# Expert weights on the sync queue in the second mixture of a gated cross-attention stack

## The chip, the cores and the metric

The kernel runs on one core of a Trainium2 chip. The metric is device time in microseconds (us) of one execution. Before the change three executions took 871.26 us in the median (871.09 to 873.1).

## The reference

The program takes 8 sequences of 100 tokens, 256 features each (T = 800 tokens), and a context of 361 rows per sequence. It applies four parts in a row, each as `x = x + tanh(gate) * part(layernorm(x))`: a cross attention, a part with attention and a mixture of experts, another cross attention, and a second mixture of experts. Only the last is touched here:

```
d2 = |x|^2 + |centroid|^2 - 2 x centroid^T          # 8 experts
w, sel = top_k(sqrt(max(d2, 1e-12)), 2);  w = softmax(w)
for e in range(8):
    h = silu(x @ Wg[e] + bg[e]) * (x @ W1[e] + b1[e])      # 256 -> 684
    out = out + we[:, e] * (h @ W2[e] + b2[e])             # 684 -> 256
```

## The kernel before

Each of the five engines (TensorE, ScalarE, VectorE, GpSimd, and SyncE, called SP, which only starts transfers) runs a list of its own, written out by hand; counting semaphores order them. The second mixture is computed by need: a token is worked on only by its two experts.

**The blocks.** The pairs of token and expert are sorted into 20 blocks of 128 slots (`NBLK`), each for one expert. Blocks 0 to 7 belong to experts 0 to 7. The 12 others (`NOV`) go to experts with more than 128 tokens; their owners are known only when the router is done. `route` (from line 2112) and `owners` (line 2199) compute on VectorE the token of each slot (XROW, for reading), the row of the output (TROW, for adding) and the owners. Line 2205 writes into WROW, for each block and partition, the row number `128 * expert + partition` in the weight tables; line 2096 does so for blocks 0 to 7 from a constant.

**The data of a block.** The gate and up weights of an expert are 128 rows of 2,736 floats, 1.40 MB, held in one of three tiles RAW. ScalarE rounds them into GUH (`gu_high`, line 1349) and VectorE writes the rest into GUL (`gu_low`, line 2072), half a tile at a time. The down weights lie in the DRAM table as 128 rows of 1,536 floats per expert, of which 115 are used (114 rows of weights, one of bias); they go to one of two tiles DOWN. Token rows (128 of 1,024 B) are gathered from a DRAM copy into XB. Result rows, 128 of 1,024 B in one of two tiles YO, are added into the output in DRAM by an indirect transfer with addition.

**One turn of TensorE's loop** (line 1027), for block k: gate and up products of half 0 (`up1`, 14 products); three transposes of the hidden part of block k-1, half 1 (`turn_hidden`, line 1011); two transposes of the tokens of block k+1 (line 981); gate and up products of half 1; the down product of block k-1 (`down1`, line 1014, 6 products that the trace shows as 12 matmuls); three transposes of block k, half 0. `down1` waits for the hidden part, for the down tile (line 1017) and for the result rows of the block before to be out of PSUM (line 1018). All matmuls are recorded with line 468, that of a helper. VectorE scales the down product into YO (`rows_out`, line 2223), and before that waits until the added rows of two blocks before have landed.

**Who moves what.** SP loads statically: the router's constants, the weights of experts 0 to 2 and the down weights of expert 0 (lines 445 to 455; tiles 1 and 2 behind a wait for the mixed heads, line 449, and the biases behind these tiles, line 453); it stores the token rows (line 457) and the first output (line 459). All else of the mixture goes through GpSimd's queue, each as an indirect transfer: `gather_weights` (line 1538, rows by WROW), `gather_down` (line 1565, 115 rows by WROW), `gather_rows` (line 1570) and `add_rows` (line 1579). GpSimd's loop (line 1596) does for each k, in this order:

```
gather_rows(k + 3)        # waits until the token rows before have landed
wait until block k's weights are split;  gather_weights(k + 3)
add_rows(k - 1)           # waits for YO, and until the added rows before have landed (line 1582)
gather_down(k + 1)
```

So the down tile of block k+1 follows, in the program and in the queue, the added rows of block k-1, whose product was the last reader of the same tile.

Of the kernel before, what the change touches and what calls it, by code (L numbers as in the profile page):

```python
# [13 lines left out]
U32 = mybir.dt.uint32  # L14
ALU = mybir.AluOpType
# [4 lines left out]
B, S, D = 8, 100, 256  # L20
# [3 lines left out]
P = 128  # L24
# [9 lines left out]
E1, HID1 = 8, 684  # L34
# [3 lines left out]
HT1 = HID1 // 6  # L38
NBLK = (2 * T + E1 * P) // P
NOV = NBLK - E1  # L40
# [12 lines left out]
def program(nc, t):  # L53

    with ExitStack() as ctx:
# [6 lines left out]
        def part(name, shape, region, at, dt=F32R):  # L62

            return nc.alloc_sbuf_tensor_at(name, shape, dt, offset=base[region] + 4 * at)
# [11 lines left out]
        RB = sb("RB", [P, 11400])  # L76
# [138 lines left out]
        at_ = GU1  # L215
        ROUTE = cut(RB, at_, 568)
        LIMITS = ROUTE[:, 0:48].rearrange("p (e j) -> p e j", e=E1)
        BEFORE = ROUTE[:, 48:112].rearrange("p (e f) -> p e f", e=E1)
        SHIFT, BLOCK, TOKEN = ROUTE[:, 112:120], ROUTE[:, 120:120 + NOV], ROUTE[0:S, 132:140]
        LANE, UNITROW, FIRST = ROUTE[:, 140:141], ROUTE[:, 141:142], ROUTE[:, 142:150]  # L220
        STATIC, PICKED = ROUTE[:, 150:158], ROUTE[:, 158:166]
        STARTS, EMPTY = ROUTE[:, 166:166 + NBLK], ROUTE[:, 186:186 + NBLK]
        LANES, TRIANGLE = ROUTE[:, 206:206 + P], ROUTE[0:S, 334:334 + S + P]
        TMP = cut(RB, at_ + 568, 288)
# [1 line left out]
        FRONT, PAST = TMP[:, 64:128].rearrange("p (e f) -> p e f", e=E1), TMP[:, 128:136]  # L226
        PASSED, OWNER = TMP[:, 136:136 + NOV * E1].rearrange("p (k e) -> p k e", e=E1), TMP[:, 232:232 + NOV]
        VACANT, OFFSET = TMP[:, 244:244 + NBLK], TMP[:, 264:272]
        WROW = part("WROW", [P, NBLK], "RB", at_ + 856, U32)
        TROW = part("TROW", [P, NBLK], "RB", at_ + 880, U32)  # L230
        XROW = part("XROW", [P, NBLK], "RB", at_ + 904, U32)
        PICKB = part("PICKB", [P, NBLK], "RB", at_ + 928)
# [120 lines left out]
        def _(sp):  # L353
            def load(dst, src, name):
                sp.dma_start(dst, src).then_inc(sem[name], 16)
# [56 lines left out]
            def load_keys(b):  # L412
                sp.wait_ge(sem[f"c_keys_stored{b % 2}"], 16 * (b // 2 + 1))
                if b >= 3:
                    sp.wait_ge(sem["c_turned_scores_summed"], 12 * (b - 2))
                if b == 2:
                    sp.wait_ge(sem["c_query_turned_up"], 16)
                src = KSC[b % 2].rearrange("(p x) n c -> x p n c", x=32)
                for r, n in enumerate((0, 0, 1)):
                    load(KST[b % 3][32 * r:32 * r + 32, :, :].bitcast(F32), src[:, :, n, :], f"c_keys_loaded{b % 3}")  # L420
                rows = 5 if b < 3 else 1
                sp.wait_ge(sem["mask_stored"], 16)
                src = MSC[16 * b:16 * b + rows].unsqueeze(1).to_broadcast([rows, 8, KVE])
                load(KST[b % 3][96:96 + rows, :, :].bitcast(F32), src, f"c_keys_loaded{b % 3}")
# [15 lines left out]
            for b in range(B - 3):  # L440
                if b + 4 < B:
                    load_context(b + 4)
                store_keys(b + 3)
                load_keys(b + 3)
            load(ROUTE, t["route"], "moe1_small_loaded")
            load(RAW[0], t["W1"][0:P], "moe1_small_loaded")
            sp.wait_ge(sem["c_turned_scores_summed"], 12 * (B - 1))
            sp.wait_ge(sem["moe1_small_loaded"], 48)
            sp.wait_ge(sem["c_heads_mixed"], 4 * (B - 1))
            for k in (1, 2):  # L450
                load(RAW[k], t["W1"][k * P:(k + 1) * P], "moe1_small_loaded")
            sp.wait_ge(sem["c_turned_scores_summed"], 12 * B)
            sp.wait_ge(sem["moe1_small_loaded"], 80)
            load(BRAW, t["b1g"], "moe1_small_loaded")
            load(DOWN[0], t["W2"][0:P].rearrange("p (t c) -> p t c", t=6), "moe1_small_loaded")
            sp.wait_ge(sem["rows_copied"], 4)
            sp.dma_start(XROWS.rearrange("(b s) c -> s b c", s=S), ROWS[:, :, :]).then_inc(sem["rows_stored"], 16)
            sp.wait_ge(sem["moe_turned_copied"], 6)
            sp.dma_start(t["out"][0:T].rearrange("(b s) c -> s b c", s=S),
                         RESID[:, :, :]).then_inc(sem["out_stored"], 16)  # L460
            sp.wait_ge(sem["out_stored"], 16)
            sp.wait_ge(sem["rows_added"], 16 * NBLK)

# [2 lines left out]
        def _(pe):  # L466
# [546 lines left out]

            def down1(k):
                pe.wait_ge(sem["hidden_high_ready"], N0 + 2 * k + 2)
                if k:
                    pe.wait_ge(sem[f"down_loaded{k % 2}"], 16 * ((k + 1) // 2))
                    pe.wait_ge(sem["rows_out_ready"], k)
                else:
                    pe.wait_ge(sem["router_result_ready"], 8)  # L1020
                for x in range(6):
                    rows = HT1 if x else HT1 + 1
                    m = mm(PS[:, 7, 0:D], HTT1[0:rows, x, :], DOWN[k % 2][0:rows, x, :], x == 0, x == 5)
                m.then_inc(sem["down_summed"], 1)
# [18 lines left out]
        def _(act):  # L1043
# [297 lines left out]
                             PS[0:96, 4 + i % 3, 0:HALF]).then_inc(sem["c_query_stacked_even"], 1)  # L1341

            def weights_there(k):
                if k >= 3:
                    act.wait_ge(sem[f"weights_loaded{k % 3}"], 16 * (k // 3))
                else:
                    act.wait_ge(sem["moe1_small_loaded"], 80 if k else 48)

            def gu_high(k, j):
                weights_there(k)  # L1350
# [64 lines left out]
                         PS[0:HT1, 5 + j, 0:3 * P].rearrange("p (x c) -> p x c",  # L1415
                                                             x=3)).then_inc(sem["hidden_high_ready"], 1)

            act.wait_ge(sem["moe1_small_loaded"], 112)
            act.wait_ge(sem["zeros_set"], 7)
            act.copy(BROWS[0:40, 0:2 * HID1], BRAW).then_inc(sem["bias_rows_ready"], 1)  # L1420
            gu_high(1, 0)
# [31 lines left out]
        def _(pool):  # L1453
# [81 lines left out]
                                       COLS[0:96, 21 + u:22 + u].unsqueeze(2).to_broadcast([96, 8, S]),  # L1535
                                       ALU.mult).then_inc(sem["c_query_slots_ready"], 1)

            def gather_weights(k):
                pool.indirect_dma_start(RAW[k % 3], None, t["W1"],
                                        bass.IndirectOffsetOnAxis(ap=WROW[:, k:k + 1],  # L1540
                                                                  axis=0)).then_inc(sem[f"weights_loaded{k % 3}"], 16)

            pool.wait_ge(sem["zeros_set"], 6)
            for b in range(3):
                mask_queries(b)
# [16 lines left out]
            pool.wait_ge(sem["c_added_to_x"], 4)  # L1562
            pool.wait_ge(sem["zeros_set"], 7)
            pool.memset(HTT1[96:P, 0, :], 1.0).then_inc(sem["zeros_set"], 1)
            def gather_down(k):
                pool.indirect_dma_start(DOWN[k % 2][0:HT1 + 1].rearrange("p t c -> p (t c)"), None, t["W2"],
                                        bass.IndirectOffsetOnAxis(ap=WROW[0:HT1 + 1, k:k + 1],
                                                                  axis=0)).then_inc(sem[f"down_loaded{k % 2}"], 16)

            def gather_rows(k):  # L1570
                if k:
                    pool.wait_ge(sem["tokens_loaded"], 16 * k)
# [10 lines left out]
                pool.indirect_dma_start(t["out"], bass.IndirectOffsetOnAxis(ap=TROW[:, k:k + 1], axis=0),  # L1583
                                        YO[:, k % 2, :], None, compute_op=ALU.add).then_inc(sem["rows_added"], 16)

            pool.wait_ge(sem["expert_weights_low_ready"], N0 + 2)
            gather_weights(3)
            gather_down(1)
            pool.wait_ge(sem["rows_stored"], 16)
            pool.wait_ge(sem["router_result_ready"], 5)  # L1590
            gather_rows(0)
# [2 lines left out]
            pool.wait_ge(sem["router_result_ready"], 6)  # L1594
            pool.wait_ge(sem["out_stored"], 16)
            for k in range(NBLK + 1):
                if k + 3 == E1:
                    pool.wait_ge(sem["router_result_ready"], 9)
                if k + 3 < NBLK:
                    gather_rows(k + 3)  # L1600
                if k and k + 3 < NBLK:
                    pool.wait_ge(sem["expert_weights_low_ready"], N0 + 2 * k + 2)
                    gather_weights(k + 3)
                if k:
                    add_rows(k - 1)
                    if k + 1 < NBLK:
                        gather_down(k + 1)


        @block.vector  # L1610
        def _(dve):
# [465 lines left out]
            for q in range(-2, QUADS):  # L2077
                b, g = divmod(q, 4)
                ahead = q + 2 < QUADS
                if ahead:  # L2080
                    top(q + 2, 0)
                    top(q + 2, 1)
                if g == 1 and b >= 1:
                    outs(b - 1)
                if g in (1, 2) and 0 <= b and b + 3 < B:
                    keys_lo(b + 3, g - 1)
                if ahead:
                    top(q + 2, 2)
                    top(q + 2, 3)
                    split_maxima(q + 2)  # L2090
                if q < 0:
                    keys_lo(2, q + 2)
                if q == 24:
                    dve.wait_ge(sem["moe1_small_loaded"], 48)
                    dve.tensor_copy(PICKB[:, 0:E1], PICKED)
                    dve.tensor_copy(WROW[:, 0:E1], STATIC).then_inc(sem["router_result_ready"], 1)
                if q == -2:
                    stack_odd(1)
            outs(B - 1)
# [99 lines left out]
            def owners():  # L2199
                link(dve.tensor_tensor(PAST, PAST, FULL, ALU.add))  # L2200
                link(dve.tensor_tensor(PASSED, BLOCK.unsqueeze(2).to_broadcast([P, NOV, E1]),
                                       PAST.unsqueeze(1).to_broadcast([P, NOV, E1]), ALU.is_ge))
                link(dve.tensor_reduce(OWNER, PASSED, AX_X, ALU.add))
                link(dve.tensor_scalar(OWNER, OWNER, E1 - 1.0, None, ALU.min))
                dve.tensor_scalar(WROW[:, E1:NBLK], OWNER, float(P), LANE, ALU.mult,
                                  ALU.add).then_inc(sem["router_result_ready"], 1)
                dve.tensor_scalar(PICKB[:, E1:NBLK], OWNER, UNITROW, None,
                                  ALU.is_equal).then_inc(sem["router_result_ready"], 1)

# [183 lines left out]
```

## Time and profile before

| | us |
|---|---|
| median of three executions | 871.26 |
| the profiled execution, its own time | 877.44 |
| its span, first to last instruction | 875.6 |
| mean granted TensorE clock, share of full | 0.933 |

| engine | busy us | share of the span |
|---|---|---|
| TensorE, products (PE) | 760.1 | 87% |
| TensorE, weight loads (PEld) | 629.0 | 72% |
| VectorE (DVE) | 563.3 | 64% |
| ScalarE (ACT) | 415.0 | 47% |
| GpSimd (POOL) | 284.2 | 32% |

The second mixture begins with its router at about 643 us; its first product starts at 667.85 us. Transfers: GpSimd's queue carried 42.51 MB over the span, SP's 41.13 MB. "issue" as the end of an idle time means that the profile shows no releaser. "DMA share" is the mean busy share of the core's 16 DMA engines. "SPq" is SP's queue; the time beside an issue there is that of the issue, or, for merged ones, from the first to the last. "x12" counts instructions. A chain is followed back from the last instruction, at each step to what released it.

### The profile page before, as it was taken

Reading aid. Unit: us, or ns where it says so; the run is one execution under the profiler, and the core shown is the slowest. Engines: PE = TensorE matmul, PEld = TensorE weight load, DVE = VectorE, ACT = ScalarE, POOL = GpSimd, SP = SyncE. Lnnn points to the kernel's source line nnn. Section 1 sums busy time; section 2 is a strip of 40 time slices with the busy share of each in tenths; the row PEclk is TensorE's granted clock in tenths of the full one; section 3 lists DMA queues with packets and bytes.
Section 4 is the critical chain, followed back from the end, with each engine's and each line's share of the span. In section 5 each row is a group of like instructions: output and inputs, shape, how many; then the busy total and the mean of one; then the engine's idle time right before and its main releaser. Section 6 shows DMA issues by size and latency. Waiting matters only on the chain.

```text
span 875.6 us, 13584 instructions
## 1 busy us (share of the span) xinstructions
PE 760.1 (87%) x4761; PEld 629.0 (72%) x4761; DVE 563.3 (64%) x1031; ACT 415.0 (47%) x896; POOL 284.2 (32%) x231
## 2 busy tenths in 40 slices
PE   6999999998988399989988988888978988888894
PEld 3588888888944387479964766676558877778783
DVE  3369999998359799176665666765365644454540
ACT  4544444442342299254443565666472544453440
POOL 0074544440016234300033022240312454554632
PEclk9999999999999699879999999997876999998998
DMA  6400000000240000000007674350432689888862
GB/s 243 173 1 18 18 18 18 18 1 0 84 191 0 0 2 2 1 0 1 10 0 176 156 169 106 108 144 21 156 134 68 190 236 231 238 225 241 237 157 67
DMA packets 33610, 84.51 MB, mean 97 GB/s; under 512 B 8566, under 2 KB 24406, under 8 KB 30215
## 3 DMA queue, kind: packets, MB, share of 16 engines
q0 software_dynamic: 13584, 42.51, 17.8%
q1 hardware_dynamic: 19959, 41.13, 15.8%
q8 instruction: 40, 0.66, 0.3%
q14 instruction: 27, 0.22, 0.1%
HBM read 73.23 MB, written 10.38 MB: 95 GB/s over the span
## 4 chain that ended last, share of the span: by engine, by line
PE 56%; DVE 13%; issue 7%; ACT 4%; DMA 2%; POOL 1%; POOLq 0%; SPq 0%; DVEq 0%; ACTq 0%
PE PS L468 52%; DVE RW L1752 2%; PE PS L1011 1%; DVE SM L2050 1%; DVE WK L1812 1%; PE PS L640 1%; DVE WK L1809 1%; DVE RO L1755 1%; DMA KST<-mask_rows 1%; PE PS L857 1%; PE PS L981 1%; ACT SQ L1056 1%; ACT RO L1189 0%; POOL OT L1551 0%; DVE M L2059 0%
## 5 line engine op out<-in xcount | busy, mean ns | idle before, releaser
L1466 POOL TENSOR_TENSOR PRODL<-RW,PRODH 128x361 fp32r<-128x361 f32 x64 | 64.9, 1017 | 114.0 <-ACT PRODH L1123 110.4
L468 PE MATMUL PS<-CTXH,WKV0H 128*128 128x362 f32 x256 | 86.4, 338 | 9.6 <-DVE RW L1708 9.0
L2050 DVE TENSOR_REDUCE SM<-PS 100x1 f32<-100x362 f32 x128 | 64.8, 531 | 44.5 <-PE PS L468 43.8
L468 PE MATMUL PS<-RB,HTT 114*128 114x256 f32 (+1 forms) x240 | 65.4, 429 | 27.3 <-issue 24.8
L468 PE MATMUL PS<-CTXL,WKV0H 128*128 128x362 f32 x256 | 84.7, 331 | 0.0
L468 PE MATMUL PS<-CTXH,WKV0L 128*128 128x362 f32 x256 | 84.3, 329 | 0.0
L468 PEld LDWEIGHTS PS<-RB,HTT 114*128 114x128 f32 (+1 forms) x240 | 50.0, 214 | 38.7 <-issue 31.0
L1312 ACT ACTIVATE WK<-PS 120x400 f32<-120x400 f32 (+1 forms) x96 | 48.4, 507 | 40.9 <-PE PS L468 40.0
L468 PEld LDWEIGHTS PS<-CTXH,WKV0H 128*128 128x128 f32 x256 | 48.7, 190 | 15.9 <-DVE RW L1708 11.1
L468 PE MATMUL PS<-KST,QST 97*100 97x362 f32 x128 | 53.2, 428 | 6.3 <-DMA KST<-mask_rows 3.4
L1755 DVE TENSOR_REDUCE RO<-RW 128x100 f32<-128x400 f32 x64 | 56.2, 878 | 2.2
L1123 ACT CAST PRODH<-RW 128x361 fp32r<-128x361 f32 x64 | 31.8, 496 | 53.8 <-DVE RW L1708 53.5
L2074 DVE TENSOR_TENSOR GUL<-RB,GUH 128x1368 fp32r<-128x1368 f32 x28 | 44.1, 1578 | 14.3 <-ACT GUH L1353 14.3
L1115 ACT COPY RW<-PS 128x361 f32<-128x361 f32 x64 | 29.5, 463 | 49.2 <-PE PS L468 47.8
L1583 POOL DMA_INDIRECT out<-YO,TROW x20 | 32.2, 1608 | 62.3 <-DVE YO L2227 30.8
L1414 ACT COPY HTT<-PS 114x384 f32<-114x384 f32 x40 | 19.2, 483 | 69.4 <-PE PS L1011 69.4
L468 PE MATMUL PS<-GUH,XTH 128*128 128x342 f32 x160 | 51.9, 324 | 0.0
L468 PE MATMUL PS<-GUL,XTH 128*128 128x342 f32 x160 | 51.8, 324 | 0.0
L468 PE MATMUL PS<-GUH,XTL 128*128 128x342 f32 x160 | 51.6, 323 | 0.0
L1551 POOL TENSOR_TENSOR OT<-STD 128x400 f32<-128x400 f32 x8 | 11.2, 1397 | 117.8 <-ACT STD L1327 117.8
L468 PEld LDWEIGHTS PS<-CTXL,WKV0H 128*128 128x128 f32 x256 | 49.0, 192 | 0.0
L468 PEld LDWEIGHTS PS<-CTXH,WKV0L 128*128 128x128 f32 x256 | 48.8, 191 | 0.0
(314 smaller groups left out, 2041.1 us busy)
## 6 DMA issues: line engine op xcount, KB each, us to landing
KST<-keys_by_head SPq DMA_DIRECT2D x24, 362.0 KB
keys_by_head<-KTHL SPq DMA_DIRECT2D x8, 724.0 KB, 3.4
CTX<-ctxT SPq DMA_DIRECT2D x16, 361.0 KB, 6.7
RB<-W SPq DMA_DIRECT2D x2, 1368.0 KB
RW<-WGU SPq DMA_DIRECT2D x1, 2304.0 KB, 8.6
RW<-WKV SPq DMA_DIRECT2D x1, 2048.0 KB, 9.8
RQ<-W SPq DMA_DIRECT2D x1, 1368.0 KB
RW<-WD SPq DMA_DIRECT2D x1, 1152.0 KB, 10.2
```

Of the source, the lines that this page charges most:

```text
L468: return pe.matmul(out, lhsT, rhs, start=start, stop=stop)
L1115: act.copy(VSB[:, i % 3, 0:KV], PS[:, 4 + i % 2, 0:KV]).then_inc(sem["a_values_copied"], 1)
L1123: act.copy(PRODH[:, i % 4, 0:KV], PROD[:, i % 3, 0:KV]).then_inc(sem["a_products_high_ready"], 1)
L1312: act.activation(PTC[0:CHT[c], q % 2, c, :], PS[0:CHT[c], 2 + c, 0:4 * S], ACT.Exp).then_inc(sem["c_exp_taken"], 1)
L1414: act.copy(HTT1[0:HT1, 3 * j:3 * j + 3, :], PS[0:HT1, 5 + j, 0:3 * P].rearrange("p (x c) -> p x c", x=3)).then_inc(sem["hidden_high_ready" ...
L1466: pool.tensor_tensor(low, raw, high, ALU.subtract).then_inc(sem["a_products_low_ready"], 1)
L1551: pool.tensor_tensor(o, UN.rearrange("p (g c) -> p g c", g=4), SUMS.rearrange("p (g c) -> p g c", g=4), ALU.mult).then_inc(sem["c_mixed_bi ...
L1583: pool.indirect_dma_start(t["out"], bass.IndirectOffsetOnAxis(ap=TROW[:, k:k + 1], axis=0), YO[:, k % 2, :], None, compute_op=ALU.add).the ...
L1752: dve.tensor_tensor(PV[:, i % 2, :], PS[:, 6 + i % 2, 0:HALF], VSB[:, i % 3, :], ALU.mult).then_inc(sem["a_weighted"], 1)
L1755: dve.tensor_reduce(OT0[:, ti, tok(b)], PV[:, i % 2, :].rearrange("p (c i) -> p i c", c=NC), AX_X, ALU.add).then_inc(sem["a_heads_mixed"], 1)
L2050: dve.tensor_reduce(SM1[:, q % 2, j:j + 1], PS[0:S, i % 2, 0:KVE], AX_X, ALU.max, negate=True).then_inc(sem["c_maximum_found"], 1)
L2074: dve.tensor_tensor(GUL[k % 2][:, :, j, :], raw_gu(k, j), GUH[k % 2][:, :, j, :], ALU.subtract).then_inc(sem["expert_weights_low_ready"], 1)
```

## The change

All expert weights of the mixture are loaded by SP with direct transfers. For blocks 0 to 7 the address is static. From block 8 on SP reads the owner's number from SBUF into a register (`value_load`) ahead of each transfer, once for the weights and once for the down tile, and takes the 128 table rows of that expert. The down tile is loaded with all 128 rows. GpSimd's queue keeps the token rows and the added rows. WROW and its constants go; VectorE writes the owners' numbers as integers into OWNED. Each RAW and DOWN tile has its own semaphore from the first load on. The waits at lines 448, 449 and 453 go or become smaller, since the router's constants alone are behind `moe1_small_loaded` now. SP's loop waits for the split of block k+1 before weights k+4, and for the down product of block k-1 before down tile k+1.

```diff
@@ SP
+            def expert_rows(table, k):
+                if k < E1:
+                    return table[k * P:(k + 1) * P]
+                e = sp.value_load(OWNED[0:1, k - E1:k - E1 + 1], min_val=0, max_val=E1 - 1)
+                return table[bass.ts(e, P)]
+
+            def load_weights(k):
+                load(RAW[k % 3], expert_rows(t["W1"], k), f"weights_loaded{k % 3}")
+
+            def load_down(k):
+                load(DOWN[k % 2].rearrange("p t c -> p (t c)"), expert_rows(t["W2"], k), f"down_loaded{k % 2}")
+
             load(ROUTE, t["route"], "moe1_small_loaded")
-            load(RAW[0], t["W1"][0:P], "moe1_small_loaded")
+            load_weights(0)
             sp.wait_ge(sem["c_turned_scores_summed"], 12 * (B - 1))
-            sp.wait_ge(sem["moe1_small_loaded"], 48)
-            sp.wait_ge(sem["c_heads_mixed"], 4 * (B - 1))
-            for k in (1, 2):
-                load(RAW[k], t["W1"][k * P:(k + 1) * P], "moe1_small_loaded")
+            load_weights(1)
+            load_weights(2)
             sp.wait_ge(sem["c_turned_scores_summed"], 12 * B)
-            sp.wait_ge(sem["moe1_small_loaded"], 80)
+            sp.wait_ge(sem["moe1_small_loaded"], 32)
             load(BRAW, t["b1g"], "moe1_small_loaded")
-            load(DOWN[0], t["W2"][0:P].rearrange("p (t c) -> p t c", t=6), "moe1_small_loaded")
+            load_down(0)
+            load_down(1)
+            sp.wait_ge(sem["expert_weights_low_ready"], N0 + 2)
+            load_weights(3)
             sp.wait_ge(sem["rows_copied"], 4)
             sp.dma_start(XROWS.rearrange("(b s) c -> s b c", s=S), ROWS[:, :, :]).then_inc(sem["rows_stored"], 16)
             sp.wait_ge(sem["moe_turned_copied"], 6)
             sp.dma_start(t["out"][0:T].rearrange("(b s) c -> s b c", s=S),
                          RESID[:, :, :]).then_inc(sem["out_stored"], 16)
+            for k in range(NBLK - 1):
+                if k + 4 == E1:
+                    sp.wait_ge(sem["router_result_ready"], 9)
+                if k + 4 < NBLK:
+                    sp.wait_ge(sem["expert_weights_low_ready"], N0 + 2 * (k + 1) + 2)
+                    load_weights(k + 4)
+                if k:
+                    sp.wait_ge(sem["down_summed"], N0 + k)
+                    load_down(k + 1)
@@ TensorE, down1
+                pe.wait_ge(sem[f"down_loaded{k % 2}"], 16 * (k // 2 + 1))
                 if k:
-                    pe.wait_ge(sem[f"down_loaded{k % 2}"], 16 * ((k + 1) // 2))
                     pe.wait_ge(sem["rows_out_ready"], k)
@@ ScalarE
             def weights_there(k):
-                if k >= 3:
-                    act.wait_ge(sem[f"weights_loaded{k % 3}"], 16 * (k // 3))
-                else:
-                    act.wait_ge(sem["moe1_small_loaded"], 80 if k else 48)
+                act.wait_ge(sem[f"weights_loaded{k % 3}"], 16 * (k // 3 + 1))
@@ GpSimd (the functions gather_weights and gather_down are removed)
-            pool.wait_ge(sem["expert_weights_low_ready"], N0 + 2)
-            gather_weights(3)
-            gather_down(1)
             for k in range(NBLK + 1):
-                if k + 3 == E1:
-                    pool.wait_ge(sem["router_result_ready"], 9)
                 if k + 3 < NBLK:
                     gather_rows(k + 3)
-                if k and k + 3 < NBLK:
-                    pool.wait_ge(sem["expert_weights_low_ready"], N0 + 2 * k + 2)
-                    gather_weights(k + 3)
                 if k:
                     add_rows(k - 1)
-                    if k + 1 < NBLK:
-                        gather_down(k + 1)
@@ VectorE
-                    dve.tensor_copy(PICKB[:, 0:E1], PICKED)
-                    dve.tensor_copy(WROW[:, 0:E1], STATIC).then_inc(sem["router_result_ready"], 1)
+                    dve.tensor_copy(PICKB[:, 0:E1], PICKED).then_inc(sem["router_result_ready"], 1)
@@ VectorE, owners
-                dve.tensor_scalar(WROW[:, E1:NBLK], OWNER, float(P), LANE, ALU.mult,
-                                  ALU.add).then_inc(sem["router_result_ready"], 1)
+                dve.tensor_copy(OWNED[:, :], OWNER).then_inc(sem["router_result_ready"], 1)
```

## Rows read from the trace of the kernel before

**Rows 1.** The page: the span

```profile
span 875.6 us, 13584 instructions
```

**Rows 2.** Stretch: length, busy us of PE, PEld, DVE, ACT, POOL, clock, DMA share, GB/s

```profile
700.00:840.00 140.00, 117.96 (x661) 107.39 (x659) 66.63 (x82) 62.98 (x98) 75.35 (x55) 0.94 0.87 234
```

**Rows 3.** Chain that ended last, start and length in us: block turns, stalls, down products

```profile
682.93 0.33 PE PS L1011 x3
...
719.87 0.33 PE PS L1011 x3
...
725.13 2.54 issue
727.66 4.50 PE PS L468 x12
...
803.73 0.33 PE PS L1011 x3
...
806.80 4.78 PE PS L468 x26
811.59 0.33 PE PS L1011 x3
...
857.30 2.84 PE PS L468 x12
...
860.93 3.67 DMA out<-YO,TROW
```

**Rows 4.** Waits in 668 to 860 us; columns: total us, times, longest

```profile
PE PS L468 <- issue: 25.8, 15, 3.9
```

**Rows 5.** Timeline of GpSimd, one turn of its loop; idle before, and releaser, in brackets

```profile
720.12 0.94 POOL L1539 DMA_INDIRECT RQ<-W,WROW  x1 [0.30 <-issue]
722.90 1.62 POOL L1583 DMA_INDIRECT out<-YO,TROW  x1 [1.83 <-DMA out<-YO,TROW]
724.82 1.18 POOL L1566 DMA_INDIRECT RB<-W,WROW  x1 [0.30 <-issue]
```

**Rows 6.** DMA issues in 680 to 845 us; last column: median us from issue to landing

```profile
RB<-W,WROW POOLq DMA_INDIRECT x26, 12.1
out<-YO,TROW POOLq DMA_INDIRECT x16, 9.9
```

**Rows 7.** Stretches of 2 us, columns as in rows 2

```profile
614.00:616.00 2.00, 1.99 (x31) 1.85 (x32) 0.89 (x2) 1.19 (x2) 0.00 (x0) 0.75 1.02 425
638.00:640.00 2.00, 1.96 (x6) 0.87 (x5) 0.38 (x1) 1.51 (x3) 0.81 (x1) 1.00 1.04 306
808.00:810.00 2.00, 2.00 (x13) 1.86 (x12) 1.13 (x1) 2.00 (x3) 0.27 (x1) 1.00 0.97 362
858.00:860.00 2.00, 2.00 (x11) 1.68 (x10) 0.00 (x0) 0.00 (x0) 0.00 (x0) 1.00 0.32 132
```

**Rows 8.** Timeline at the end of the kernel, all engines

```profile
854.54 1.17 POOL L1566 DMA_INDIRECT RB<-W,WROW  x1 [0.31 <-issue]
...
860.49 0.86 ACT L1414 COPY HTT<-PS 114x384 f32<-114x384 f32 x2 [4.83 <-PE PS L1011]
...
863.23 4.52 PE L468 MATMUL PS<-RB,HTT 115*128 115x256 f32 x12 [2.45 <-DMA RB<-W,WROW]
...
868.55 1.56 POOL L1583 DMA_INDIRECT out<-YO,TROW  x1 [6.03 <-DVE YO L2227]
```

**Rows 9.** Timeline of VectorE, the end of a block without a stall

```profile
810.79 1.57 DVE L2074 TENSOR_TENSOR GUL<-RB,GUH 128x1368 fp32r<-128x1368 f32 x1
```

**Rows 10.** Timeline of the sync queue: issues, with the time until the next

```profile
573.01 37.68 SPq L355 DMA_DIRECT2D RB<-W  x2
610.73 0.43 SPq L355 DMA_DIRECT2D RQ<-W  x1
...
645.59 0.31 SPq L457 DMA_DIRECT2D token_rows<-ROWS  x1
```

**Rows 11.** DMA issues of the whole span, the smallest store of the sync queue

```profile
mask_rows<-MKR SPq DMA_DIRECT2D x1, 181.0 KB, 2.1
```

More of the change, by code:

```diff
@@ L219, in program @@
         SHIFT, BLOCK, TOKEN = ROUTE[:, 112:120], ROUTE[:, 120:120 + NOV], ROUTE[0:S, 132:140]
-        LANE, UNITROW, FIRST = ROUTE[:, 140:141], ROUTE[:, 141:142], ROUTE[:, 142:150]
-        STATIC, PICKED = ROUTE[:, 150:158], ROUTE[:, 158:166]
+        UNITROW, FIRST = ROUTE[:, 141:142], ROUTE[:, 142:150]
+        PICKED = ROUTE[:, 158:166]
         STARTS, EMPTY = ROUTE[:, 166:166 + NBLK], ROUTE[:, 186:186 + NBLK]
@@ L228, in program @@
         VACANT, OFFSET = TMP[:, 244:244 + NBLK], TMP[:, 264:272]
-        WROW = part("WROW", [P, NBLK], "RB", at_ + 856, U32)
+        OWNED = part("OWNED", [P, NOV], "RB", at_ + 856, U32)
         TROW = part("TROW", [P, NBLK], "RB", at_ + 880, U32)
@@ L1416, in hidden_high @@
                                                              x=3)).then_inc(sem["hidden_high_ready"], 1)
-            act.wait_ge(sem["moe1_small_loaded"], 112)
+            act.wait_ge(sem["moe1_small_loaded"], 48)
             act.wait_ge(sem["zeros_set"], 7)
@@ L1536, in mask_queries @@
                                        ALU.mult).then_inc(sem["c_query_slots_ready"], 1)
[L1538 to L1541, printed above, removed]
             pool.wait_ge(sem["zeros_set"], 6)
@@ L1564, in _ @@
             pool.memset(HTT1[96:P, 0, :], 1.0).then_inc(sem["zeros_set"], 1)
[L1565 to L1568, printed above, removed]
             def gather_rows(k):
@@ L2093, in _ @@
                 if q == 24:
-                    dve.wait_ge(sem["moe1_small_loaded"], 48)
-                    dve.tensor_copy(PICKB[:, 0:E1], PICKED)
-                    dve.tensor_copy(WROW[:, 0:E1], STATIC).then_inc(sem["router_result_ready"], 1)
+                    dve.wait_ge(sem["moe1_small_loaded"], 32)
+                    dve.tensor_copy(PICKB[:, 0:E1], PICKED).then_inc(sem["router_result_ready"], 1)
                 if q == -2:
@@ L2369 @@
     route[0:S, 132:140] = np.arange(B) * S + np.arange(S)[:, None] + 1
-    route[:, 140] = np.arange(P)
     route[:, 141] = -1.0
@@ L2373 @@
     route[:, 142:150] = P * np.arange(E1)
-    route[:, 150:158] = P * np.arange(E1) + np.arange(P)[:, None]
     route[0:E1, 158:166] = route[32:32 + E1, 158:166] = np.eye(E1)
```

## The prediction

> **What bounds the kernel now.** I read the page first: a span of 875.6 us [rows 1]. The profiled execution took 877.44 us by its own time, 6.2 us above the median of 871.26. The change touches only the second mixture, so I then read the chain of waits from 640 us on. It is TensorE nearly throughout, and in the mixture it repeats one pattern per block. The row of three transposes that follows the down product marks a turn: turn 1 stands at 682.93, and turn 19 comes when the last down product but one ends, at 857.30 + 2.84 = 860.14 [rows 3]. That is 18 blocks in 177.2 us, 9.85 us each. Where nothing is late a block takes 811.59 - 803.73 = 7.86 us [rows 3], in which TensorE does not pause. So about 2 us of every block is lost.
>
> The loss sits in front of the down product: 15 waits of 25.8 us in all [rows 4], for instance 2.54 us at 725.13 [rows 3]. "Issue" means that no releaser shows. The program gives one: line 1017 waits for down_loaded. The last block names it too (2.45 us, released by DMA into RB) [rows 8]. The stalls cost twice: the product behind the one at 725.13 takes 4.50 us against 2.84 [rows 3], TensorE having sat idle just before. 25.8 us of waits and as much as 1.7 us behind each of the five or six longest make most of the 18 x 1.99 = 35.8 us.
>
> Why is the down tile late? GpSimd issues it behind the added rows, which wait for the previous added rows to land: 720.12 weights, 722.90 added rows, 724.82 down tile [rows 5]. The product of two blocks before ended at 719.87 [rows 3], so 6.1 us pass until this issue ends. Then it needs a median of 12.1 us to land [rows 6]. The DMA engines look full, share 0.87, but move only 234 GB/s [rows 2]. Weights loaded alone move at 425 GB/s with share 1.02 [rows 7]. The last down tile, issued at 854.54, explains this [rows 8]: while it moves alone the share is 0.32 and the rate 132 GB/s [rows 7]. 0.32 is 5 engines of 16. Its 115 rows of 6,144 B (0.707 MB) take 0.707 MB / 132 GB/s = 5.4 us on five engines. Those also carry their part of the 1.40 MB of weights (3.3 us at 425 GB/s) and of the token and added rows, so five engines set the pace while the others queue up around them.
>
> The Trainium skill, "DMA: Bandwidth & Descriptors", section "Why a DMA increments its semaphore by 16 and not by 1", has the rule: the engines used are the largest number up to 16 that divides the outer dimension. By it 115 rows give 5 and 128 give 16; the first agrees with 0.32.
>
> **The change part by part.**
> *Down tile by SP, 128 rows instead of 115.* Bytes rise to 0.786 MB. I take it to use all 16 engines, as the 128-row weights do at share 1.02 [rows 7]. At 425 GB/s a block's two tiles need 3.3 + 1.85 = 5.2 us. Token and added rows are 0.26 MB more, 0.6 us at that rate. That is 5.8 us of DMA in a block of 7.86. Bounds: 425 GB/s, and the present 234 / 0.87 = 269 GB/s, where the 2.45 MB take 9.1 us. I take the first, because the low rate belongs to the five-engine tile: in stretches of the same loop where little of it is in flight the rate is 362 [rows 7].
>
> *Order on SP.* SP now waits for the low parts, issues weights k+4, waits for the down product and issues tile k+1. Without a stall the product ends at 806.80 + 4.78 = 811.58 [rows 3] and the low parts at 810.79 + 1.57 = 812.36 [rows 9], so both go out together, weights first. From block 8 on each issue is preceded by a register read. The trace has none. Bounds: zero, and the 1.62 us of GpSimd's issue with 128 row numbers [rows 5]; I take 1.0, nearer to its 0.94 [rows 5]. Then the tile is issued 0.8 + 2 x (1.0 + 0.4) = 3.6 us after the product (0.43 an issue [rows 10]). The weights, sent 1.4 us earlier, still need 1.9 us, the tile 1.85, and landing about 2 (2.1 for a small store [rows 11]): 9.4 us. It is needed 2 x 7.86 - 2.84 = 12.9 us after the product. Even with reads of 1.62 us it takes 10.6. Nothing waits. If that cover went, each us past 12.9 would cost 0.5 us a block.
>
> *Weights by SP.* Tile k+4 goes out when block k+1 is split, some two blocks ahead of its first reading: cost zero, hidden by those two blocks, 15.7 us, against 9 us for read, issue, transfer and landing. SP's part of both waits blocks only SP, behind which stand only later loads and the final waits.
>
> *GpSimd loses 36 issues* (17 of 0.94 us or more, 19 of 1.18 [rows 5, 8]). None is on TensorE's chain; token rows are gathered three blocks ahead. Added rows must land before the next are issued. They take 9.9 us now, behind weights in the same queue [rows 6]; on a queue of their own I expect between 3.67 (alone) and 3.7 + 5.2 = 8.9, with both tiles in front on every engine. The 3.67 is the last but one, issued at 860.93 into an empty queue [rows 3]. I take 6. This is under 7.86, so it is hidden by the block.
>
> *Ahead of the loop.* Tiles 1 and 2 no longer wait for the mixed heads at 610.73 and go out up to 37 us sooner [rows 10]; line 1421 reads them first, behind the last normalization. Weights 3, which GpSimd sends so early that they move at 638 to 640 [rows 7], enter SP's queue before the token rows of 645.59 [rows 10] and need 3.3 us, so these are not held. Nothing gained or lost. A cast of WROW goes and one multiply becomes a copy: below 0.3 us, behind TensorE.
>
> *The end.* The last product waits 2.45 us and takes 4.52 [rows 8]. Its operands are ready at 860.49 + 0.86 = 861.35, so it should run 861.4 to 864.2 and the last added rows go out at about 865.2, 5.1 us behind the product before, not 8.4 (868.55 - 860.14). That is 3.3 us. The added rows before, issued at 860.93 [rows 3], have landed by then.
>
> **Sum.** 18 x (9.85 - 7.86) = 35.8, and 3.3: 39.1 us. I take off 2.8 us, 0.15 a block, because the first blocks after the change of loads and a late added row will leave some short waits. So 36.3 us, and 877.44 becomes 841.1. From the median, 871.26 - 36.3 = 835.0 if the 6.2 us between it and the profiled execution lie elsewhere, 841 if they are stalls of this loop that the other executions did not have. I take a third of them there: 837.
>
> **Rivals.**
> *A, DMA stays the limit.* The low rate is not from the five engines but from mixing two tiles and small rows. For it: share 0.87, and 306 GB/s for the lone gather of tile 3 against 425 [rows 7]. Against it: 362 in the loop. Then 9.1 us a block: 18 x 0.75 + 3.3 = 16.8 us, 854.5 from the median. Added rows that land in 8.9 us each give nearly the same.
> The Trainium skill, same page, section "Issuing engines are not separate DMA queues", speaks against the change: all issuers share the same 16 engines, and another issuer saves only issue time. By that rule alone the time would be that of this rival. It leaves out that the change also alters the row count.
>
> *B, added rows set the pace, slower.* They now compete on every engine with full-length weight rows instead of standing in order. The wait at line 1582 chains them: block time is landing time. It decides when landing passes 9.85 us. Price at the present rate: 3.7 us plus 2.19 MB / 269 GB/s = 8.1, so 11.8 a block, 18 x 1.95 = 35 us more, 903 less the end's 3. Against it: in a block of 7.86 they would have to meet every byte at the low rate.
>
> *C, the stalls are not the down tile's.* The label is only "issue". Then the time stays within 2 us of 871. Against it: added rows and product rows are done long before in every stall I read.
>
> **How the numbers follow.** Forecast 0.75, A 0.17, B 0.05, C 0.03. This kernel's measurement tells 0.3%, 2.6 us. Faster are the first two, 0.92; same is C, 0.03; slower B, 0.05. The range: below, no stall and all 6.2 us elsewhere, 871.3 - 39 = 832, and 3 us for stages whose spread I cannot see: 829. Above it takes in A: 857. B and C stay outside.
>
> **What would show it.** Right: stretches of 2 us with a share near 1 move 350 GB/s or more; turns stand about 7.9 us apart; no down product waits and none takes 4.5 us; TensorE's granted clock in the loop is 1.00. Wrong: waits move to the added rows (line 1582) or to TensorE's weights (GUH); the interval from turn 8 on is longer than before it, which would be the register reads; or the share stays near 0.9 at 270 GB/s, rival A.

## The result, and the profile after

The changed kernel takes 836.44 us in the median of four executions (836.17 to 837.66), against 872.18 us before, measured beside it. The ratio is 0.9593, 95% interval 0.9574 to 0.9611: 4.1% faster. The profiled execution took 836.42 us. The forecast was 837.0, range 829 to 857.

The page of the kernel after: its span and its transfers by queue (q1 is SP's, q0 GpSimd's).

```profile
span 834.2 us, 13705 instructions
...
q1 hardware_dynamic: 25143, 79.89, 29.1%
q0 software_dynamic: 3840, 5.25, 3.0%
```

The queues have changed places: SP's now carries 79.89 MB, GpSimd's 5.25 of its 42.51.

Stretches of the loop, columns as in rows 2:

```profile
700.00:800.00 100.00, 100.00 (x612) 94.83 (x611) 61.66 (x77) 57.59 (x89) 39.06 (x26) 1.00 0.91 313
783.00:785.00 2.00, 2.00 (x14) 1.79 (x13) 2.00 (x3) 0.45 (x2) 1.05 (x1) 1.00 0.95 365
788.00:790.00 2.00, 2.00 (x14) 1.94 (x13) 0.81 (x2) 2.00 (x4) 1.57 (x1) 1.00 1.01 421
```

This answers [rows 2]. TensorE is busy for all of 100 us, at a granted clock of 1.00 instead of 0.94, the full 2.4 GHz (over the same 100 us the kernel before had 0.93, a share of 0.87 and 233 GB/s). The share of DMA has hardly moved (0.91, before 0.87), but it now stands for 313 GB/s instead of 234, and stretches of 2 us reach 421. One share, two rates: the share says how long packets were under way, not how fast they moved.

The chain that ended last, turns as in [rows 3]:

```profile
682.16 0.33 PE PS L1033 x3
...
690.05 0.33 PE PS L1033 x3
```

```profile
807.88 0.33 PE PS L1033 x3
...
815.73 0.33 PE PS L1033 x3
```

```profile
818.58 4.81 PE PS L490 x26
...
824.17 3.52 DMA out<-YO,TROW
```

Turn 1 stands at 682.16 (before 682.93), turn 19 is the end of the down product, 818.58 + 4.81 = 823.39. That is 18 blocks in 141.2 us, 7.85 each, where the one block without a stall of [rows 3] had 7.86. After turn 19 come 10.8 us to the end of the span, before 15.5. The last added rows, as in [rows 8]:

```profile
828.45 1.54 POOL L1592 DMA_INDIRECT out<-YO,TROW  x1 [2.73 <-DVE YO L2224]
```

Waits in 668 to 834 us, as in [rows 4]:

```profile
POOL out L1592 <- PE PS L1003: 45.6, 10, 7.1
...
POOL out L1592 <- DMA out<-YO,TROW: 23.8, 5, 6.1
...
DVE YO L2224 <- DMA out<-YO,TROW: 3.7, 1, 3.7
...
PE PS L490 <- issue: 1.0, 1, 1.0
...
PE PS L490 <- ACT HTT L1433: 0.6, 1, 0.6
```

TensorE's 25.8 us of waits have become 1.6, of which one (1.0) stands ahead of the first block and one (0.6) ahead of the last product. The 2.45 us ahead of the last product, which are not in the 25.8, are this 0.6. GpSimd waits for added rows to land as before (23.8 us; before 22.8), and TensorE is busy meanwhile.

DMA issues in 680 to 810 us, last column median us to landing, as in [rows 6]:

```profile
RB<-W SPq DMA_DIRECT2D x10, 1368.0 KB, 6.0
RB<-W SPq DMA_DIRECT2D x17, 768.0 KB, 7.2
...
out<-YO,TROW POOLq DMA_INDIRECT x17, 7.1
```

The down tile (768 KB) lands 7.2 us after its issue, although it stands behind 1.40 MB of weights. Before it took 12.2; the 12.1 of [rows 6] is the median of weight and down gathers together. Added rows land in 7.1, not 9.9.

The time by place, in spans (875.6 to 834.2, 41.4 us): 0.8 ahead of turn 1, 36.0 in the 18 blocks, 4.6 behind turn 19.

### The profile page after: what moved, and what is told of

Same layout as the page of the kernel before. It is cut to its first block, busy times and chain, and to the rows that moved or that the text cites. A ratio compares the mean times of both kernels' runs of the same rounds, so it can differ in the third digit from the quotient of the medians.

```text
span 834.2 us, 13705 instructions
## 1 busy us (share of the span) xinstructions
PE 745.0 (89%) x4761; PEld 621.0 (74%) x4761; DVE 562.8 (67%) x1030; ACT 414.6 (50%) x896; POOL 241.5 (29%) x195
## 3 DMA queue, kind: packets, MB, share of 16 engines
q1 hardware_dynamic: 25143, 79.89, 29.1%
q0 software_dynamic: 3840, 5.25, 3.0%
## 4 chain that ended last, share of the span: by engine, by line
PE 55%; DVE 14%; issue 4%; ACT 3%; DMA 2%; POOL 1%; POOLq 0%; SPq 0%; DVEq 0%; ACTq 0%
PE PS L490 51%; PE PS L1033 1%; DVE SM L2049 1%; DVE WK L1811 1%; DVE RW L1751 1%; PE PS L662 1%; DVE WK L1808 1%; DMA KST<-mask_rows 1%; DVE RO L1754 1%; PE PS L879 1%; PE PS L1003 1%; ACT SQ L1078 1%; POOL OT L1565 0%; DVE M L2058 0%; DMA out<-YO,TROW 0%
## 5 line engine op out<-in xcount | busy, mean ns | idle before, releaser
L490 PE MATMUL PS<-RB,HTT 114*128 114x256 f32 (+1 forms) x240 | 55.2, 379 | 0.6 <-ACT HTT L1433 0.6
L490 PEld LDWEIGHTS PS<-RB,HTT 114*128 114x128 f32 (+1 forms) x240 | 44.7, 189 | 6.2 <-ACT HTT L1433 0.9
L1707 DVE TENSOR_TENSOR RW<-PS,RQ 128x400 f32<-128x400 f32 x64 | 36.2, 567 | 8.4 <-PE PS L490 7.5
```

The lines of the kernel that those rows point to most:

```text
L490: return pe.matmul(out, lhsT, rhs, start=start, stop=stop)
L1707: dve.tensor_tensor(out, k, q, ALU.mult).then_inc(sem["a_products_ready"], 1)
```

## Experiments

The change has two halves: another issuer with another order, and 128 rows for 115. The first runs take them apart. "Before" beside each is the median of the kernel before on the same chip.

**One half alone: 128 rows, all else as before.**

```diff
-                pool.indirect_dma_start(DOWN[k % 2][0:HT1 + 1].rearrange("p t c -> p (t c)"), None, t["W2"],
-                                        bass.IndirectOffsetOnAxis(ap=WROW[0:HT1 + 1, k:k + 1],
+                pool.indirect_dma_start(DOWN[k % 2][0:128].rearrange("p t c -> p (t c)"), None, t["W2"],
+                                        bass.IndirectOffsetOnAxis(ap=WROW[0:128, k:k + 1],
```

> The kernel before with one edit: GpSimd's gather of the down tile moves 128 rows instead of 115; issuer, queue and order stay. Five-engine theory: the tile spreads over 16 engines (0.786 MB at 425 GB/s is 1.85 us, not 5.4), issued 6.1 us behind the product it lands about 10 us behind it, under the 12.9 that TensorE leaves; blocks of 7.9 to 8.4 us, time 836 to 847. Theory of the queue (the gain comes from taking the weights off GpSimd's queue): the stalls stay, and 11% more bytes make it 870 to 875.

Measured: 839.1 us, before 875.51, ratio 0.9587 (0.9538 to 0.9635). As expected by the five-engine theory (836 to 847). Changing one number, 115 to 128, gives the whole gain within the interval; issuer and order had no part in it that these runs can tell from noise. The stretch 700 to 800 us, columns as in rows 2, and TensorE's waits in 668 to 840 us:

```profile
700.00:800.00 100.00, 98.72 (x599) 93.19 (x598) 60.88 (x76) 57.22 (x89) 67.84 (x50) 1.00 0.94 302
```

```profile
PE PS L468 <- issue: 1.3, 2, 0.8
```

GpSimd still issues everything, 50 transfers in this stretch, and TensorE waits 1.3 us.

**The other half alone: weights by SP, the down tile still 115 rows by GpSimd.**

```diff
+            sp.wait_ge(sem["expert_weights_low_ready"], N0 + 2)
+            load_weights(3)
...
+            for k in range(4, NBLK):
+                if k == E1:
+                    sp.wait_ge(sem["router_result_ready"], 9)
+                sp.wait_ge(sem["expert_weights_low_ready"], N0 + 2 * (k - 3) + 2)
+                load_weights(k)
...
-            gather_weights(3)
...
-                if k and k + 3 < NBLK:
-                    pool.wait_ge(sem["expert_weights_low_ready"], N0 + 2 * k + 2)
-                    gather_weights(k + 3)
```

> The kernel before with half of the change: SP loads the gate and up weights of blocks 3 to 19 (owner's number from a register), GpSimd goes on gathering the down tile with 115 rows, on five engines in turn. Theory: the five-engine tile stays late. Its issue ends some 5 us behind the product (one issue fewer before it), it needs 5.4 us alone and 8 to 10 beside weights, so the pair of blocks takes (5 + 9 + 2.84) us = 8.4 a block at best and 9.5 with landings of 11: 846 to 866, so most of the change's 36 us missing. Theory of the queue (taking 1.40 MB a block out of GpSimd's queue is the gain): 836 to 842.

Measured: 880.88 us, before 874.22, ratio 1.0085 (1.0052 to 1.0118). This missed: it is 0.9% slower, where I expected 846 to 866. Its DMA issues in 700 to 800 us, and GpSimd's timeline:

```profile
RB<-W,WROW POOLq DMA_INDIRECT x9, 11.4
```

```profile
736.63 1.21 POOL L1582 DMA_INDIRECT RB<-W,WROW  x1 [0.30 <-issue]
745.49 0.97 POOL L1591 DMA_INDIRECT XB<-token_rows,XROW  x1 [7.64 <-DMA XB<-token_rows,XROW]
748.64 1.62 POOL L1599 DMA_INDIRECT out<-YO,TROW  x1 [2.18 <-DVE YO L2240]
```

The down tile still lands after 11.4 us. In this turn GpSimd then stands idle for 7.64 us until the token rows sent before have landed, and so issues the next added rows late. It is the longest such wait; between 700 and 800 us they are six of ten, 33.3 us in all. TensorE's waits are in sum what they were (28.0 us, before 28.2, with those of the last product). What costs the 0.9% was not separated.

**The whole change, but 115 rows.**

```diff
-                load(DOWN[k % 2].rearrange("p t c -> p (t c)"), expert_rows(t["W2"], k), f"down_loaded{k % 2}")
+                rows = HT1 + 1
+                load(DOWN[k % 2][0:rows].rearrange("p t c -> p (t c)"), expert_rows(t["W2"], k)[0:rows],
+                     f"down_loaded{k % 2}")
```

> The kernel after with one edit: SP loads 115 rows of the down tile instead of 128. Five-engine theory: 5.4 us for the tile and 3.3 for the weights plus 0.6 for rows on the same five engines, 9.3 to 9.9 us a block: 862 to 873. Theory of the queue: time stays at 836 to 840.

Measured: 898.2 us, before 875.51, ratio 1.0265 (1.0211 to 1.0319). The direction is that of the five-engine theory, but the size missed, by 25 us over the upper bound of 873: the time goes past the kernel before. 13 rows more or less turn the same change from 4.1% faster to 2.7% slower. TensorE's waits in 668 to 900 us, the stretch with columns as in rows 2, and two turns of the chain:

```profile
PE PS L492 <- issue: 41.5, 14, 5.3
```

```profile
700.00:800.00 100.00, 78.09 (x414) 70.53 (x413) 40.14 (x50) 38.31 (x61) 23.20 (x18) 0.90 0.74 202
```

```profile
682.13 0.33 PE PS L1035 x3
...
865.71 2.85 PE PS L492 x12
```

Turn 1 stands at 682.13, turn 17 at 868.56: 11.7 us a block, where the sum of loads on five engines said 9.3 to 9.9. The runs with 11 and 16 small rows below take up why it is slower than from GpSimd.

**One row more in the kernel before: 116.** (The edit is that of the first run, with 116 and likewise 119 and 120 in the next ones.)

> The kernel before with one edit: the gather of the down tile moves 116 rows instead of 115, one row more. By the engine count as the largest divisor up to 16, 116 rows use 4 engines, not 5: 0.713 MB at 106 GB/s is 6.7 us, 1.3 us more than now, so blocks of about 11.2 us and 890 to 900 in all. If only the bytes counted (0.9% more), 871 to 873.

Measured: 904.2 us, before 875.51, ratio 1.034 (1.0277 to 1.0403), just above the 890 to 900 expected. DMA issues over the span:

```profile
RB<-W,WROW POOLq DMA_INDIRECT x31, 15.0
```

Gathers land after 15.0 us instead of 11.8. One row in 115 costs 29 us: it is how the rows divide, not the bytes. The records of single packets in the traces show the engines: between 700 and 800 us exactly four rows of the down tile are under way for 72% of the time, with 115 rows exactly five for 61%.

**119 rows, 7 engines.**

> The kernel before, the gather of the down tile with 119 rows = 7 x 17: by the largest divisor, 7 engines. 0.731 MB at 7/16 of 425 GB/s take 3.9 us, between the 1.85 of 128 rows (839.1) and the 5.4 of 115 (875.5); 116 rows with 6.7 us took 904.2, so each us less of the tile is worth some 22 us until TensorE is the limit: 838 to 852. If only the bytes or another threshold count, 872 or more.

Measured: 876.97 us (ten executions), before 874.67, ratio 1.0025 (0.9994 to 1.0055). This missed. Seven engines are no better than five:

```profile
700.00:800.00 100.00, 82.71 (x456) 74.96 (x455) 47.97 (x58) 43.03 (x67) 51.59 (x40) 0.93 0.96 232
```

The share is 0.96, the rate 232 GB/s. Exactly seven rows of the down tile are under way for 52% of this stretch, so it does run on seven engines. But each row takes longer: a down row of 6,144 B takes 437 ns in the mean, with 115 rows 339. An engine's part of the tile, as an estimate, is then 17 rows x 0.437 = 7.4 us, with 115 rows 23 x 0.339 = 7.8 us: nearly the same. The tile lands after 12.3 us, with 115 rows after 12.2. Even with no weight row beside it a down row takes 346 ns here, with 115 rows 253. And the weights are slower too: a weight row of 10,944 B that starts while seven down rows are under way takes 875 ns in the mean, against 439 with none; beside five of 115 rows it was 724. So a tile on part of the engines goes together with slower weight rows on the others. Why, no run shows.

**120 rows, 15 engines.**

> The kernel before, the gather of the down tile with 120 rows = 15 x 8. The run with 119 rows (7 engines) missed its expectation: no faster than 115 rows, and beside its 7 packets the weights' packets took 869 ns, beside the 5 of 115 rows 712, alone 434. If the number of engines decides in the end, 15 engines are as good as 16: 838 to 845. If what decides is that a tile that is not spread over all 16 slows the weights beside it, the stalls stay: 860 to 880.

Measured: 841.05 us, before 871.43, ratio 0.9673 (0.9609 to 0.9738), as expected. Nearly all of the gain is back. The rate over the same stretch is 295 GB/s at a share of 1.00, and the gathers land in 9.1 us.

```profile
700.00:800.00 100.00, 98.58 (x595) 92.33 (x594) 59.99 (x75) 57.01 (x88) 67.47 (x50) 1.00 1.00 295
```

**115 rows in two transfers, 112 and 3, in the kernel after.**

```diff
+                src = expert_rows(t["W2"], k)
+                for lo, hi in ((0, 112), (112, HT1 + 1)):
+                    load(DOWN[k % 2][lo:hi].rearrange("p t c -> p (t c)"), src[lo:hi], f"down_loaded{k % 2}")
...
-                pe.wait_ge(sem[f"down_loaded{k % 2}"], 16 * (k // 2 + 1))
+                pe.wait_ge(sem[f"down_loaded{k % 2}"], 32 * (k // 2 + 1))
```

> The kernel after with the 115 used rows of the down tile loaded by SP in two transfers, of 112 and of 3 rows. Five-engine theory: 112 rows divide by 16, 1.6 us on all engines, the 3 rows next to nothing: 836 to 839, as with 128 rows. Rival: the 115 rows are slow for another reason than how they divide (fewer partitions, a partial tile): 885 or more.

Measured: 838.74 us, before 874.67, ratio 0.9594 (0.9555 to 0.9633): as expected, and as the change with 128. The same 115 rows are cheap once 112 of them divide by 16.

**Does the set of engines move on?** Both edits act on the kernel before, once per block, with n = 11 or 16 (the semaphore was freed by letting two early loads share one):

```diff
+            def move_cursor(i):
+                if i:
+                    pool.wait_ge(sem["cursor_moved"], 16 * i)
+                pool.indirect_dma_start(RANK[0:n, 0:8], None, t["rank"],
+                                        bass.IndirectOffsetOnAxis(ap=WROW[0:n, 0:1],
+                                                                  axis=0)).then_inc(sem["cursor_moved"], 16)
...
                         gather_down(k + 1)
+                        move_cursor(k - 1)
```

> The kernel before; behind each gather of the down tile GpSimd gathers 11 rows of 32 B more, which nobody reads. Theory: GpSimd's transfers on fewer than 16 engines take the next engines in turn, SP's always the same ones, which is why the same 115 rows cost 898 from SP and 875 from GpSimd. 5 + 11 = 16 brings the turn back to the same place, so the down tile always meets the same five engines: 895 to 915. If there is no such turn: as the run with 16 rows.

> Control for the run with 11 rows: 16 rows of 32 B, on all engines, which leave the turn where it is. It shows what the additional issue (1.2 us of GpSimd a block) costs by itself: 875 to 885 in either theory.

Measured: 904.11 us with 11 rows, ratio 1.0382 (1.033 to 1.0433), as expected; 868.68 with 16 rows, ratio 0.9986 (0.9959 to 1.0014), before 871.43. The control was expected at 875 to 885: its additional issue costs nothing that can be seen. A dummy gather costs 3.8% with 11 rows (352 bytes) and nothing with 16 (512 bytes). Waits of TensorE in 668 to 920 us, first with 11, then with 16:

```profile
PE PS L469 <- issue: 44.8, 16, 4.6
```

```profile
PE PS L469 <- issue: 20.1, 14, 3.9
```

There is a rival: a transfer on 11 engines could cost the time by itself, as it lands late (12.0 us after its issue, with 16 rows 8.7) and holds up GpSimd's next one. No run tried this apart, but the packet records speak for the engines. Counted over 700 to 800 us, the packets under way at one instant are:

| | exactly ten | exactly five |
|---|---|---|
| kernel before | 11.7% of the time | 2.3% |
| with 16 small rows | 11.3% | 3.8% |
| weights by SP, down tile by GpSimd | 9.9% | 14.4% |
| with 11 small rows | 1.9% | 21.7% |
| whole change, 115 rows by SP | 1.6% | 25.3% |

Ten at once fit two sets of five: the new down tile on one, and on another the weight rows that the tile before has delayed. With 116 rows the peak is at eight (16.9%), with 119 at fourteen (12.9%). Where ten are rare and five frequent, the delayed weight rows are on the same five engines that the next tile needs; in the third run both occur. By this GpSimd's five engines move on with each tile, and SP takes the same ones each time; held in one place they cost about the same from either (1.0382 and 1.0265). The trace does not number the engines: this is read from counts. The Trainium skill, "DMA: Bandwidth & Descriptors", section "Why a DMA increments its semaphore by 16 and not by 1", says both: the lowest-numbered ones for SP's kind of transfer, a round-robin cursor for GpSimd's.

**Register reads, twice and five times as many, in the kernel after.**

```diff
+                for _ in range(4):          # in the other run once
+                    sp.value_load(OWNED[0:1, k - E1:k - E1 + 1], min_val=0, max_val=E1 - 1)
                 e = sp.value_load(OWNED[0:1, k - E1:k - E1 + 1], min_val=0, max_val=E1 - 1)
```

> The kernel after with one more register read ahead of each read: 1.5 us more on the path of the down tile, inside the 3.1 us to spare: 836 to 838. If each read showed in the time: 12 blocks x 1.5 / 2 = 9 us more.

> The kernel after with four more register reads ahead of each read (blocks 8 to 19, weights and down tile). In the trace of after a read takes about 0.75 us, the down tile is issued 2.7 us behind the product and lands 7.1 later: 9.8 of 12.9 us, 3.1 us to spare. Eight more reads between two down tiles put 6.0 us in: 2.9 too many, 1.45 a block for some 10 blocks, so 848 to 856. If the reads lie elsewhere than on this path: 836 to 839.

Measured: 837.33 us with two reads (ratio 0.9574, 0.9538 to 0.961), as expected, and 840.91 with five (ratio 0.9606, 0.9578 to 0.9633), where I had expected 848 or more. SP's issues in a block with five reads, weights and then the down tile:

```profile
767.23 0.34 SPq L355 DMA_DIRECT2D RB<-W  x1
```

```profile
770.56 0.34 SPq L355 DMA_DIRECT2D RB<-W  x1
```

```profile
RB<-W SPq DMA_DIRECT2D x1, 768.0 KB, 4.8
```

The last line is the down tile of the block before. From the issue of the weights to that of the tile five reads take 770.56 - 767.23 - 0.34 = 3.0 us. In after, with one read, the two issues are:

```profile
785.85 1.46 SPq L355 DMA_DIRECT2D RB<-W  x2
```

That leaves 1.46 - 2 x 0.34 = 0.78 us, so each further read takes 0.55, and eight of them 4.4 us where I had reckoned with 6.0. The tile also lands sooner after its issue, 6.0 us in the median of 720 to 810 us against 7.0 in after: it used to spend the difference in the queue behind the weights, and a later issue eats that first. I had added the two. TensorE waits 3.4 us in this run, 1.0 of them ahead of the first block as in after; the median is 3.6 us above that of two reads on the same chip.

**The kernel before once more.**

> The kernel before, unchanged, once more with a profile: where do the 6.2 us lie by which the profiled execution of before was above the median? If in the loop, turn 1 stands at 682 to 683 us again and turn 19 comes 170 to 173 us later, not 177.2. If ahead of the loop, turn 1 stands some 5 us earlier and the 18 blocks take 177 us again.

Measured: span 869.6 us, by its own time 873.2 (one execution, on another chip).

```profile
680.66 0.33 PE PS L1011 x3
```

```profile
847.80 4.79 PE PS L468 x26
...
853.39 4.21 DMA out<-YO,TROW
```

Turn 1 stands at 680.66, turn 19 at 852.60: 171.9 us of loop against 177.2, as expected if the difference lies in the loop; but turn 1 also comes earlier. Of the 6.0 us between the two spans, 5.3 lie in the loop and 2.3 ahead of it, and 1.5 go the other way behind it.

## Why the prediction was right, and where two steps were not

**Right: the place and its price.** The loss stood in front of the down product, and there it went: 18 blocks in 141.2 us against a forecast of 141.5 at 7.86 each. The second price of a stall, the slower product behind it, went too. Before, the product of 4.50 us behind the stall at 725.13 ran at a granted clock of 0.62 (columns as in rows 2):

```profile
727.66:732.16 4.50, 4.50 (x14) 3.69 (x15) 0.83 (x1) 0.00 (x0) 2.29 (x2) 0.62 0.80 205
```

In the loop of after the granted clock is 1.00 throughout 700 to 800 us.

**Right in the main: the cause.** "Five engines" was read from a share of 0.32. The runs with 116, 120, 128 and 112 + 3 rows bear out that it matters how the rows divide, and the two halves tried alone exclude the queue. The run with 119 rows shows that the number of engines alone does not give the time. Rival A held that the low rate comes from mixed traffic on any number of engines; with 128 rows the traffic is as mixed and moves at 302 to 313 GB/s. The issuer saved nothing here, with 128 rows (0.9587 without it, 0.9593 with it); with 115 rows it was not even neutral. Rivals B and C did not come: added rows land after 7.1 us, and the stalls are gone with the tile.

**Wrong: "five engines set the pace" as a sum of loads on the same five.** That sum (5.4 + 3.3 us and rows) presumes that the five are the same in every block. With GpSimd they were not (11 against 16 rows). The path of one tile fits better: 6.1 us to its issue's end, 12.1 to landing and 2.84 of product, two blocks long, 10.5 us a block from medians where 9.85 was measured. Of the 12.1 some 7.8 us are the tile's rows (23 on an engine at 339 ns); the rest was not separated. Where the engines are fixed, the sum is of the right kind, but too small. In the run with SP's 115 rows exactly five packets are under way for a quarter of 700 to 800 us, and never fewer: five engines that do not pause. But a block takes 11.7 us there, not 9.3 to 9.9. The rate of 132 GB/s in the 5.4 us is that of a tile alone. In this run a down row takes 317 ns in the mean, 239 with no weight row beside it. By an estimate, 23 rows of 317 ns instead of 5.4 us add 1.9 us, which is most of the difference. And the sum left out that each row's time depends on what runs beside it and on how the rows divide, which is why 7 engines did not help.

**Wrong, and cancelled: the corrections to the sum.** I took off 2.8 us for short waits that would remain; in the loop none did. The end gave 4.6 us, not 3.3, and the part ahead of turn 1 gave 0.8. Without the 2.8 the sum is 877.44 - 39.1 = 838.3, 1.9 us above what the profiled execution of after took (836.42); with them it was 841.1, 4.7 above. The other 1.3 and 0.8 us bring the 838.3 to 836.2. Against that, I laid a third of the 6.2 us between the profiled execution and the median into the loop. The second profile has 5.3 us less loop than the first, some 3 us more than my third. If the median executions are like it, 41.0 us of the profiled one leave 35.7 for the median, and 872.18 - 836.44 is 35.7. That this holds for all of them is not shown. The two errors have opposite signs: that 837.0 came within 0.6 us is luck.

**Small steps.** At the end, the last added rows go out 828.45 - 823.39 = 5.1 us behind the product before, as forecast; the 1.3 us on top lie behind that issue (5.7 us to the end of the span, before 7.05), where I had looked for nothing. The register read, guessed at 1.0 us with nothing in the trace, takes 0.55 to 0.78. The down tile was to be there 9.4 us behind the product; after SP's 2.6 us and 7.2 to landing it is 9.8, of 12.9. (The 10.6 us with reads of 1.62 us should read 10.0, since the weights then have 2.0 us of lead instead of 1.4; nothing hung on it.) Added rows, taken at 6 between 3.67 and 8.9, take 7.1.

## What to carry to other kernels

Look at the number of partitions of each transfer before asking who issues it: with 115, 116 or 119 rows the tile ran on 5, 4 or 7 of the 16 DMA engines here, and padding it to a multiple of 16, or splitting off the odd rows, can be worth more than a new queue. A transfer that runs alone shows it at once: here a share of 0.32 at 132 GB/s, 26 GB/s an engine, as with all 16 at 425. Moving such a tile from GpSimd to SP made it worse here: with the weights by SP already, the ratio went from 1.0085 to 1.0265.

A share of 0.9 is no proof that the bytes need the time: compare its GB/s with the best stretch of the same trace. And where profiled execution and median differ, a second profile is cheaper than a guess about where the difference lies.

## What was not expected of the hardware

- GpSimd's down tile on five engines takes other engines each time, read from the counts above. 352 bytes in 11 rows, which bring it back to the same place, cost 3.8%; 512 bytes in 16 rows nothing.
- While a down tile moves on 5 or 7 engines, weight rows on the others are slower: 724 and 875 ns, against 437 and 439 with no down row under way. Why was not settled. The Trainium skill, same page, section "Back-pressure in remote DMA", tells of saturated SBUF ports that hold up the source engines and others that share the path; it speaks of another kind of transfer. No run here shows the ports.
- The time of one down row depends on how many rows the tile has, even with no weight row under way: 246 ns in the kernel after (128 rows) and 253 in the kernel before (115), but 346 with 119, 373 with 120 and 361 with 112 + 3 rows. No run says why.
